# A decoder layer on one core: norms with a negated mean, and fewer products of ones at the start

## The chip, the cores and the metric

The kernel runs on one core of a Trainium2 chip. The metric is the device time of one execution in microseconds (us), as the median of several runs; lower is better. The core has five engines that run side by side, each in its own order: TensorE (PE; its weight loads are listed apart as PEld), VectorE (DVE), ScalarE (ACT), GpSimd (POOL) and SyncE (SP), whose work here is to issue DMAs. ACT issues a few DMAs too. Semaphores hold the engines together.

## The reference

One decoder layer over x of shape (4, 512, 128), all in float32: causal self-attention with 16 heads of 8, cross-attention over a context of 77 rows, and a mixture of 8 experts of which each token takes 2. A norm without gain or bias stands in front of each of the three.

```
def _layernorm(x, axis=-1, eps=1e-05):
    m = jnp.mean(x, axis=axis, keepdims=True)
    v = jnp.var(x, axis=axis, keepdims=True)
    return (x - m) / jnp.sqrt(v + eps)
...
x = x + attn(_layernorm(x), Wq, bq, Wk, bk, Wv, bv, Wp, bp)          # causal, softmax
x = x + xattn(_layernorm(x), ctx, ctx, mask, Wq, Wk, Wv, Wo)         # softmax over 77
x = x + ffn(_layernorm(x), gate_W, gate_b, expert_W, expert_b)       # top 2 of 8, /2
```

So there are 3 norms for each of 4 batches, 12 in all.

## The kernel before

**Layout.** A batch (b) is 512 tokens, in T = 4 tiles of 128 tokens on the partitions with 128 features in a row. `state` holds x for all batches and takes every residual sum. PSUM is one tensor `banks` of 8 banks; a step of the schedule gets one bank or two.

**Order of the work.** Each step is a triple (kind, b, k). `chains()` writes the steps as chains, one letter each: "a" is the first half of batch 0 (first_stats, first_norm, first_turn, first_q, first_k, first_split_q, first_split_k, then project_v and add_bias), "q" the same for its second half, "b", "c", "d" the norm and projections of batches 1 to 3, "e" to "h" the peaks (row maxima of the scores) of batches 0 to 3, "s" the scores, "v" the values, and so on. The string `ORDER` names which chain takes its next step; each engine walks through the same list `SCHEDULE` and issues what a step asks of it. So the string sets the order on all engines, and no engine passes a step that it waits in. The letter "w" is a step of its own, `warm`: one product of ones, 128x512 in bf16, into a bank that nobody reads (line 893). It takes time on PE alone and keeps it busy.

**A norm.** For a step ln_stats (11 of the 12 norms) DVE takes bn_stats of the four tiles (line 740) and bn_aggr (line 743), which leave mean and variance side by side in `moments`, and signals `moments_ready`. POOL adds epsilon to the variance (`var`, line 483) and raises it to the power of minus one half (`rstd`, line 484). For ln_norm POOL makes `normed`, tile by tile, in one tensor_scalar with two column operands (line 493):

```
for t in range(T):
    last = gp.tensor_scalar(normed[:, i % 2, t], state[:, b, t], moments[:, n, t, 0:1],
                            rstd[:, n, t:t + 1], ALU.subtract, ALU.mult)
```

PE then turns the four tiles (turn_x, line 884), ACT copies them out as `normed_t` (line 613), and the projections follow. The first norm of batch 0 is split in two halves of two tiles: DVE's statistics (lines 748 and 751), POOL's `var` and `rstd` (lines 472 and 473), and the two tiles by DVE for half 0 (line 757), by POOL for half 1 (line 477).

**The start.** POOL fills `ones_b` (line 438) and PE begins with 29 warm products, since these stand ahead of the first turn (first_turn, line 912) in the string. Then come the turn of half 0, 2 more, first_q of half 0 (line 918), the turn of half 1, first_k of half 0, 1 more, first_q of half 1, 2 more, first_k of half 1, project_v (line 877), the context's keys (line 896) and 30 more. ACT and DVE split q and k into bf16 parts (lines 621 to 627, 766, 773), SP and ACT copy these by DMA into `q_stack` and `k_stack` (line 339), and the peaks begin: products (lines 962 and 967) that DVE reduces to maxima (line 781). The scores (line 1008) wait for those maxima to be turned, copied (line 662) and written into `q_stack` by SP (line 415). SP issues all its DMAs in the order of the steps.

Of the kernel before, what the change touches and what calls it, by code (L numbers as in the profile page):

```python
# [11 lines left out]
ALU = mybir.AluOpType  # L12
# [3 lines left out]
B, S, D, H, E = 4, 512, 128, 16, 8  # L16
DH = D // H
S2 = 77
T = S // 128
# [5 lines left out]
LN_EPS = 1e-5  # L25
# [26 lines left out]
def chains():  # L52
# [37 lines left out]
    "aqaqPVPPPwwwwwwwwwwwwwwwwwwwwwwwwwwwwwaLLLbwwaPLqaPwqwwaqbaVcqaqKwwwwwwwwwwwwwwwwwwwwwwwwwwwwwweeebe"  # L90
    "cebebebPebwweeewwbcKeewKKeKwwweeKiewwwwwKeeicecefwsLesiwwsfsfsafswfisfsfsfsvfsvfssvvfsjsvvmbsfsdvjsf"
    "svfscvvfsfvsfdsmvmcffscmdfsfmvfjsmsmLmvsggjvsgvsgmgsgmgsgvsmgvsgndggksdgvsgsvAkAsvAsnsAvgsAvAdsgvnAs"
    "AnAsggvdgnsgvsgAsvgsknshsnvcxhxvxkhxvhoynxhxyxhnEhshnhxhdsholsEnshsvlhsyshsvvBsBdyBPEsBvBPsEsBvBBBvs"
    "hoEhshoBEshsvEoEshxoxhsovxohxyxhxyFxvloElsoEsxFEvsvosssvpyyssvvFspsvCsFsCvCCCvvpCCFCEpFzCFzpCtpFptzx"
    "xtxpxzypFxxypFxFxGytGpyttGGFwwwwzwwwwDtDGDDtDDwDDDGzGtzDtztxGGxxGxGyxxyxxtHytyHtHGHwwzHztHtHztzHwwww"
    "wHwwwHHtttwwwwwwwwwwwwwwHwwwwzztttztztttt"
# [76 lines left out]
def decoder_layer(nc, x, ctx_t, mask, wq, bq, wk, bk, wv, bv, wp, bp, xwq, xwk, xwv, xwo,  # L173
                  gate_w, gate_b, expert_w, expert_b, out):
    with ExitStack() as stack:
        def sb(name, shape, dt=F32):
            return stack.enter_context(nc.sbuf_tensor(name, shape, dt))
# [28 lines left out]
        moments = sb("moments", [128, 3 * B, T, 2])  # L206
        var = sb("var", [128, 3 * B, T])
# [221 lines left out]
        def _(pool):  # L429
            gp = nc.gpsimd  # L430
# [36 lines left out]
            for step in SCHEDULE:  # L467
                kind, b, k = step
                if kind == "first_stats":
                    t = slice(2 * k, 2 * k + 2)  # L470
                    pool.wait_ge(first_moments_ready, k + 1)
                    link(gp.tensor_scalar(var[:, 0, t], moments[:, 0, t, 1], LN_EPS, None, ALU.add))
                    gp.tensor_tensor(rstd[:, 0, t], var[:, 0, t], minus_half[:, t], ALU.pow).then_inc(first_rstd_ready, 1)
                elif kind == "first_norm" and k == 1:
                    pool.wait_ge(first_rstd_ready, 2)
                    for t in (2, 3):
                        last = gp.tensor_scalar(normed[:, 0, t], state[:, 0, t], moments[:, 0, t, 0:1],
                                                rstd[:, 0, t:t + 1], ALU.subtract, ALU.mult)
                    last.then_inc(first_norm_ready[k], 1)
                elif kind == "ln_stats":  # L480
                    n = 3 * b + k
                    pool.wait_ge(moments_ready, STATS[step])
                    link(gp.tensor_scalar(var[:, n], moments[:, n, :, 1], LN_EPS, None, ALU.add))  # L483
                    link(gp.tensor_tensor(rstd[:, n], var[:, n], minus_half[:], ALU.pow))  # L484
                elif kind == "ln_norm":
# [6 lines left out]
                    for t in range(T):  # L492
                        last = gp.tensor_scalar(normed[:, i % 2, t], state[:, b, t], moments[:, n, t, 0:1],  # L493
                                                rstd[:, n, t:t + 1], ALU.subtract, ALU.mult)
# [210 lines left out]
        def _(dve):  # L705
# [10 lines left out]
            for step in SCHEDULE:  # L716
# [16 lines left out]
                elif kind == "ln_stats":  # L733
# [10 lines left out]
                    last.then_inc(moments_ready, 1)  # L744
# [384 lines left out]
```

## Time and profile before

| | before |
|---|---|
| median of 3 runs | 279.18 us |
| lowest and highest run | 278.38, 280.30 us |
| the profiled execution, device time | 278.69 us |
| its span, first to last instruction | 277.0 us |
| busy: PE, DVE, ACT, POOL | 258.9, 207.6, 162.7, 150.5 us |
| TensorE clock granted, mean | 0.994 |
| chain that ended last: PE, DVE, POOL, ACT | 64%, 17%, 11%, 3% |

The span is 1.7 us shorter than the device time of the same execution. The chain that ended last is followed back from the last instruction, at each step to what released it or to the instruction before it on its engine. An engine's idle time is put down to whatever ended it.

### The profile page before, as it was taken

The page shows a single profiled execution, that of the slowest core. Times are in us where ns is not written, and L with a number is a line of the kernel's source. Part 1 is how long each engine was busy: PE and PEld are TensorE (multiplying, and loading weights), DVE is VectorE, ACT ScalarE, POOL GpSimd, SP SyncE. Part 2 cuts the span into 40 slices and gives each one's busy share as a digit, 9 for nine tenths or more (in the row PEclk, how much of TensorE's full clock was granted, in tenths as well). Part 3 has the DMA queues.
Part 4 walks back from the last instruction along what each step waited for, and adds up shares of the span by engine and source line. Part 5 has one row for each costly group of instructions (what it writes and reads, how often), then busy time and mean ns, then how long its engine had stood idle before and what let it go on. Part 6 is the DMA issues. An engine that isn't in the chain of part 4 may idle for free.

```text
span 277.0 us, 6747 instructions
## 1 busy us (share of the span) xinstructions
PE 258.9 (93%) x2642; PEld 140.3 (51%) x2642; DVE 207.6 (75%) x406; ACT 162.7 (59%) x223; POOL 150.5 (54%) x266
## 2 busy tenths in 40 slices
PE   8999896899988999999999969999799999998993
PEld 2554442434544444453545525367455684586583
DVE  6489997867887989987979945899338973864651
ACT  4232624989866988799977979961592009501100
POOL 7999833758869665675667694625811070032000
PEclk9999999799999999999999999999999999999999
DMA  3453364000452313400310001300004100100101
GB/s 106 110 143 94 86 165 110 2 6 4 117 152 71 82 37 105 135 9 5 100 31 2 7 2 29 98 2 8 0 11 116 38 7 2 38 2 0 38 2 39
DMA packets 21635, 14.62 MB, mean 53 GB/s; under 512 B 2788, under 2 KB 21604, under 8 KB 21604
## 3 DMA queue, kind: packets, MB, share of 16 engines
q1 hardware_dynamic: 20324, 13.61, 18.1%
q10 hardware_dynamic: 1280, 0.59, 0.8%
q8 instruction: 21, 0.34, 0.5%
q14 instruction: 10, 0.08, 0.1%
HBM read 2.39 MB, written 1.05 MB: 12 GB/s over the span
## 4 chain that ended last, share of the span: by engine, by line
PE 64%; DVE 17%; POOL 11%; ACT 3%; issue 2%; DMA 1%; POOLq 0%; SPq 0%; ACTq 0%
PE banks L1024 12%; POOL normed L493 8%; PE banks L1087 7%; PE banks L893 7%; PE banks L1008 7%; DVE peaks L781 6%; PE banks L884 5%; PE banks L967 4%; PE banks L1046 4%; PE banks L877 4%; PE banks L962 3%; DVE xpeaks L788 3%; POOL rstd L484 2%; PE banks L1073 2%; PE banks L1035 2%
## 5 line engine op out<-in xcount | busy, mean ns | idle before, releaser
L781 DVE TENSOR_REDUCE peaks<-banks 128x2 f32<-128x1024 f32 (+3 forms) x88 | 95.2, 1122 | 16.4 <-PE banks L967 15.8
L672 ACT ACTIVATE probs<-banks 128x1024 f32<-128x1024 f32 x80 | 79.4, 1031 | 14.3 <-PE banks L1008 13.7
L569 POOL TENSOR_SCALAR_AFFINE_SELECT probs<-probs 128x512 f32<-128x512 f32 (+1 forms) x80 | 43.2, 545 | 35.2 <-ACT probs L672 35.1
L1024 PE MATMUL banks<-probs,v_s 128*32 128x256 f32 (+3 forms) x512 | 43.2, 440 | 0.0
L677 ACT ACTIVATE xprobs<-banks 77x1024 f32<-77x1024 f32 x32 | 31.0, 1017 | 9.7 <-PE banks L1035 9.6
L493 POOL TENSOR_SCALAR normed<-state,moments,rstd 128x128 f32<-128x128 f32 x44 | 35.0, 809 | 0.7
L893 PE MATMUL banks<-ones_b 128*128 128x512 bf16 x118 | 32.1, 411 | 2.4 <-POOL minus_half L439 1.4
L1008 PE MATMUL banks<-q_stack,k_stack 64*128 64x512 bf16 (+3 forms) x256 | 30.8, 306 | 3.0 <-DMA q_stack<-peaks_t 2.4
L1087 PEld LDWEIGHTS banks<-expert_w_s,scaled 128*128 128x128 f32 x256 | 29.6, 192 | 4.9 <-issue 4.6
L1087 PE MATMUL banks<-expert_w_s,scaled 128*128 128x128 f32 x256 | 32.1, 280 | 0.0
L967 PE MATMUL banks<-k_stack,q_stack 64*128 64x512 bf16 (+3 forms) x256 | 31.9, 301 | 0.0
L851 DVE TENSOR_TENSOR scaled<-banks,normed_t 128x1024 f32<-128x1024 f32 x16 | 19.4, 1218 | 10.5 <-PE banks L1073 10.4
L962 PE MATMUL banks<-causal,halves 64*128 64x128 bf16 (+3 forms) x352 | 26.0, 227 | 1.0 <-DVE peaks L781 0.8
L788 DVE TENSOR_REDUCE xpeaks<-banks 128x8 f32<-128x616 f32 x32 | 23.9, 792 | 1.9 <-PE banks L983 1.6
L962 PEld LDWEIGHTS banks<-causal,halves 64*128 64x128 bf16 x352 | 13.3, 96 | 23.2 <-DVE peaks L781 10.4
L893 PEld LDWEIGHTS banks<-ones_b 128*128 128x128 bf16 x118 | 11.7, 104 | 17.4 <-issue 5.5
L1024 PEld LDWEIGHTS banks<-probs,v_s 128*32 128x32 f32 x512 | 12.3, 108 | 15.5 <-issue 11.4
L1008 PEld LDWEIGHTS banks<-q_stack,k_stack 64*128 64x128 bf16 x256 | 9.9, 96 | 16.3 <-DVE peaks L781 4.8
L1046 PE MATMUL banks<-xprobs,xv_s 77*32 77x512 f32 x128 | 16.6, 602 | 0.0
L613 ACT COPY normed_t<-banks 128x512 f32<-128x512 f32 x11 | 6.2, 586 | 16.3 <-PE banks L884 16.3
L807 DVE TENSOR_TENSOR g_scores<-banks,gate_b_s 128x32 f32<-128x32 f32 x4 | 0.8, 192 | 19.1 <-PE banks L877 19.1
L483 POOL TENSOR_SCALAR var<-moments 128x4 f32<-128x4 f32 x11 | 2.7, 246 | 22.4 <-DVE moments L743 22.3
(172 smaller groups left out, 370.8 us busy)
## 6 DMA issues: line engine op xcount, KB each, us to landing
xq_stack<-parts_x SPq DMA_DIRECT2D x24, 128.0 KB, 2.4
q_stack<-parts_q SPq DMA_DIRECT2D x18, 128.0 KB, 2.5
k_stack<-parts_k SPq DMA_DIRECT2D x18, 128.0 KB, 2.5
out<-state SPq DMA_DIRECT2D x4, 256.0 KB, 2.2
state<-in_x SPq DMA_DIRECT2D x3, 256.0 KB, 2.9
q_stack<-parts_q SPq DMA_DIRECT2D x12, 64.0 KB, 2.0
expert_w_s<-in_expert_w SPq DMA_DIRECT2D x1, 512.0 KB, 4.4
xk_stack<-parts_x SPq DMA_DIRECT2D x6, 77.0 KB
```

Source lines behind the costliest of these rows:

```text
L493: last = gp.tensor_scalar(normed[:, i % 2, t], state[:, b, t], moments[:, n, t, 0:1], rstd[:, n, t:t + 1], ALU.subtract, ALU.mult)
L569: gp.affine_select(out=v, in_=v, compare_op=ALU.is_ge, fill=0.0, base=0, pattern=pattern, channel_multiplier=-1).then_inc(causal_done, 1)
L672: ac.activation(probs[:, grp % 2, u], two_banks(step), ACT.Exp, scale=SCALE).then_inc(taken_by_act, 1)
L677: ac.activation(xprobs[0:S2, n % XPROBS], two_banks(step)[0:S2], ACT.Exp, scale=SCALE).then_inc(taken_by_act, 1)
L781: ve.tensor_reduce(peaks[:, f, t, :, a:a + n], two_banks(step)[:, :, 0:n * width].rearrange("p s (h k) -> p s h k", h=n), X_AXIS, ALU.max, ...
L788: ve.tensor_reduce(xpeaks[:, t, :, a:a + n], two_banks(step)[:, :, 0:n * S2].rearrange("p s (h k) -> p s h k", h=n), X_AXIS, ALU.max, nega ...
L893: te.matmul(bank(step), ones_b[:, 0:128], ones_b[:], start=True, stop=True)
L962: te.matmul(diagonal[:, s, :, 64 * i:128], halves[r, i], causal[r, 0:n, 0:128 - 64 * i], start=(i == 0), stop=False, skip_group_check=True)
L967: last = te.matmul(two[:, s, width * h:width * h + width], q_stack[r, b % 2, 4 * f + a + h, 128 * t:128 * t + 128], k_stack[r, b % 2, 4 * ...
L1008: last = te.matmul(two[:, s, col:col + n], k_stack[r, b % 2, p, 128 * kt:128 * kt + 128], q_stack[r, b % 2, p, 128 * kt:S], start=True, st ...
L1024: last = te.matmul(home[32 * c:32 * c + 32, 128 * kt:S], weight.rearrange("p a b -> p (a b)"), probs[:, half, unit, c % 2, col:col + S - 1 ...
L1087: last = te.matmul(home[:, D * t:D * t + D], scaled[:, (4 * b + k) % SCALED, i, 128 * t:128 * t + 128], expert_w_s[:, 2 * k + i], start=Fa ...
```

## The change

It has three parts. First, the norms that POOL makes add a negated mean in place of subtracting the mean: a new tile `shift` holds the means times -1, and line 493's operation (495 in the changed kernel) reads state, `shift` and `rstd` with ALU.add and ALU.mult. Second, for the 11 norms of ln_stats DVE makes both `shift` and the sum of variance and epsilon, `var`, behind its bn_aggr, after a wait for the last of these, and signals `moments_ready` with `var`; POOL no longer makes `var` there. In first_stats POOL still makes `var`, and for half 1 `shift` too. DVE's own two tiles of half 0 still subtract. Third, `ORDER` has 14 products of ones ahead of the first turn where it had 29, none between first_q and first_k of half 1 where it had 2, 4 behind the first three peaks, and 2, 1 and 2 more in three late places: 110 in all where it had 118. All other letters stand in the same order.

```
@@ ORDER @@
-    "aqaqPVPPPwwwwwwwwwwwwwwwwwwwwwwwwwwwwwaLLLbwwaPLqaPwqwwaqbaVcqaqKwwwwwwwwwwwwwwwwwwwwwwwwwwwwwweeebe"
+    "aqaqPVPPPwwwwwwwwwwwwwwaLLLbwwaPLqaPwqaqbaVcqaqKwwwwwwwwwwwwwwwwwwwwwwwwwwwwwweeewwwwbecebebebPebwwe"
...
+        shift = sb("shift", [128, 3 * B, T])
...
                 if kind == "first_stats":
                     t = slice(2 * k, 2 * k + 2)
                     pool.wait_ge(first_moments_ready, k + 1)
+                    if k == 1:
+                        gp.tensor_scalar(shift[:, 0, t], moments[:, 0, t, 0], -1.0, None, ALU.mult)
                     link(gp.tensor_scalar(var[:, 0, t], moments[:, 0, t, 1], LN_EPS, None, ALU.add))
...
                     for t in (2, 3):
-                        last = gp.tensor_scalar(normed[:, 0, t], state[:, 0, t], moments[:, 0, t, 0:1],
-                                                rstd[:, 0, t:t + 1], ALU.subtract, ALU.mult)
+                        last = gp.tensor_scalar(normed[:, 0, t], state[:, 0, t], shift[:, 0, t:t + 1],
+                                                rstd[:, 0, t:t + 1], ALU.add, ALU.mult)
...
                     pool.wait_ge(moments_ready, STATS[step])
-                    link(gp.tensor_scalar(var[:, n], moments[:, n, :, 1], LN_EPS, None, ALU.add))
                     link(gp.tensor_tensor(rstd[:, n], var[:, n], minus_half[:], ALU.pow))
...
                     for t in range(T):
-                        last = gp.tensor_scalar(normed[:, i % 2, t], state[:, b, t], moments[:, n, t, 0:1],
-                                                rstd[:, n, t:t + 1], ALU.subtract, ALU.mult)
+                        last = gp.tensor_scalar(normed[:, i % 2, t], state[:, b, t], shift[:, n, t:t + 1],
+                                                rstd[:, n, t:t + 1], ALU.add, ALU.mult)
...
                     for t in range(T):
                         last = ve.bn_aggr(moments[:, n, t], stats[:, n, t])
-                    last.then_inc(moments_ready, 1)
+                    link(last)
+                    ve.tensor_scalar(shift[:, n], moments[:, n, :, 0], -1.0, None, ALU.mult)
+                    ve.tensor_scalar(var[:, n], moments[:, n, :, 1], LN_EPS, None, ALU.add).then_inc(moments_ready, 1)
```

On PE, at the program's start, this stood before (ident and normed are the turns, ones_b the products of ones):

```order
L893 MATMUL banks<-ones_b 128x512 x29
L912 MATMUL banks<-ident,normed 128x128 x2
L893 MATMUL banks<-ones_b 128x512 x2
L918 MATMUL banks<-normed_t,wq_s 128x256
L912 MATMUL banks<-ident,normed 128x128 x2
L918 MATMUL banks<-normed_t,wk_s 128x256
L893 MATMUL banks<-ones_b 128x512
L918 MATMUL banks<-normed_t,wq_s 128x256
L893 MATMUL banks<-ones_b 128x512 x2
L918 MATMUL banks<-normed_t,wk_s 128x256
```

And this stands there in the changed kernel, whose lines are numbered 4 higher:

```order
L897 MATMUL banks<-ones_b 128x512 x14
L916 MATMUL banks<-ident,normed 128x128 x2
L897 MATMUL banks<-ones_b 128x512 x2
L922 MATMUL banks<-normed_t,wq_s 128x256
L916 MATMUL banks<-ident,normed 128x128 x2
L922 MATMUL banks<-normed_t,wk_s 128x256
L897 MATMUL banks<-ones_b 128x512
L922 MATMUL banks<-normed_t,wq_s 128x256
L922 MATMUL banks<-normed_t,wk_s 128x256
```

Fifteen products are gone ahead of the first turn and two ahead of the last first_k; the rest keeps its order.

On DVE, at the statistics of batch 1 near the start, this stands in the changed kernel:

```order
L742 BN_STATS stats<-state 128x6 x4
L745 BN_AGGR moments<-stats 128x2 x4
L747 TENSOR_SCALAR shift<-moments 128x4
L748 TENSOR_SCALAR var<-moments 128x4
L770 SCALAR_TENSOR_TENSOR full_q<-banks,bq_s,parts_q 128x256
```

Before, full_q stood right behind the BN_AGGR. On POOL the same norm and the next one read, before:

```order
L483 TENSOR_SCALAR var<-moments 128x4
L484 TENSOR_TENSOR rstd<-var,minus_half 128x4
L513 MEMSET zeros_b 24x512
L513 MEMSET expert_b_s 32x512
L493 TENSOR_SCALAR normed<-state,moments,rstd 128x128 x4
L483 TENSOR_SCALAR var<-moments 128x4
L484 TENSOR_TENSOR rstd<-var,minus_half 128x4
```

and in the changed kernel:

```order
L486 TENSOR_TENSOR rstd<-var,minus_half 128x4
L515 MEMSET zeros_b 24x512
L515 MEMSET expert_b_s 32x512
L495 TENSOR_SCALAR normed<-state,shift,rstd 128x128 x4
L486 TENSOR_TENSOR rstd<-var,minus_half 128x4
```

The `var` of each norm has gone from POOL to DVE, 11 times.

## Rows read from the trace of the kernel before

**Rows 1.** Chain that ended last, in order of time (start us, us, what)
```profile
1.37 9.33 PE banks L893 x29
...
12.08 0.22 PE banks L912 x2
...
47.12 0.39 PE banks L1008 x2
```
**Rows 2.** Instructions in order of time, 5 to 24 us (start us, us, engine line)
```profile
6.25 1.59 POOL L477 TENSOR_SCALAR normed<-state,moments,rstd 128x128 f32<-128x128 f32 x2
...
7.30 2.90 PEld L893 LDWEIGHTS banks<-ones_b 128*128 128x128 bf16 x14 [0.26 <-issue]
...
8.65 0.38 DVE L743 BATCH_NORM_AGGREGATE moments<-stats 128x2 f32<-128x6 f32 x4
...
12.62 0.48 DVE L766 SCALAR_TENSOR_TENSOR full_q<-banks,bq_s,parts_q 128x256 f32<-128x256 f32 x1 [3.60 <-ACT parts_q L621]
...
15.72 6.64 PE L893 MATMUL banks<-ones_b 128*128 128x512 bf16 x30
...
18.57 3.75 POOL L493 TENSOR_SCALAR normed<-state,moments,rstd 128x128 f32<-128x128 f32 x4
...
23.05 3.48 DVE L781 TENSOR_REDUCE peaks<-banks 128x8 f32<-128x1024 f32 x3
...
23.71 0.66 PE L884 MATMUL banks<-ident,normed 128*128 128x128 f32 x4
```
**Rows 3.** Busy time by stretch (us, PE, PEld, DVE, ACT, POOL, PEclk, DMA share, GB/s)
```profile
23.00:38.00 15.00, 13.52 (x144) 7.08 (x140) 14.99 (x16) 6.92 (x15) 11.43 (x14) 1.00 0.34 90
50.00:51.00 1.00, 1.00 (x14) 0.65 (x10) 0.91 (x1) 0.88 (x2) 0.77 (x4) 0.50 0.07 16
```
**Rows 4.** SP's queue in order of time, 12 to 46 us
```profile
12.66 3.83 SPq L339 DMA_DIRECT2D q_stack<-parts_q  x6
...
44.27 1.54 SPq L415 DMA_DIRECT2D q_stack<-peaks_t  x2
```
**Rows 5.** Who waited for whom (us in total, times, longest us)
```profile
PE banks L884 <- POOL normed L493: 6.3, 6, 2.0
```
**Rows 6.** Groups of POOL by form (count | busy us, mean ns | idle before)
```profile
L493 POOL TENSOR_SCALAR normed<-state,moments,rstd 128x128 f32<-128x128 f32 x44 | 35.0, 809 | 0.7
L530 POOL TENSOR_TENSOR state<-state,bias 128x512 f32<-128x512 f32 x4 | 5.1, 1270 | 0.1
L458 POOL TENSOR_TENSOR full_q<-full_q,parts_q 128x512 f32<-128x512 f32 x3 | 3.5, 1155 | 5.4 <-ACT full_q L648 5.4
L441 POOL TENSOR_SCALAR_AFFINE_SELECT ident<-ident 128x128 f32<-128x128 f32 x1 | 0.3, 296 | 0.2 <-POOL ident L440 0.2
```
**Rows 7.** A norm's hand-over from DVE to POOL, 154 to 157 us
```profile
154.80 0.38 DVE L743 BATCH_NORM_AGGREGATE moments<-stats 128x2 f32<-128x6 f32 x4
...
155.27 0.23 POOL L483 TENSOR_SCALAR var<-moments 128x4 f32<-128x4 f32 x1
...
155.59 1.04 POOL L484 TENSOR_TENSOR rstd<-var,minus_half 128x4 f32<-128x4 f32 x1
```
**Rows 8.** DVE and POOL in the gate's step, 204 to 210 us
```profile
204.79 0.18 DVE L809 TENSOR_SCALAR g_scores<-g_scores 128x32 f32<-128x32 f32 x1
205.01 0.19 DVE L811 TENSOR_REDUCE g_max<-g_scores 128x4 f32<-128x32 f32 x1
...
208.38 1.16 POOL L464 TENSOR_TENSOR parts_x<-full_x,parts_x 128x512 bf16<-128x512 f32 x1 [2.29 <-ACT parts_x L652]
...
208.66 0.92 DVE L828 TENSOR_TENSOR g_tied<-g_left,g_top 128x32 f32<-128x32 f32 x1
```
**Rows 9.** PE at the late turns of norms (200 to 252 us)
```profile
200.07 1.06 PE L884 MATMUL banks<-ident,normed 128*128 128x128 f32 x8 [1.49 <-POOL normed L493]
...
229.09 0.63 PE L884 MATMUL banks<-ident,normed 128*128 128x128 f32 x4 [0.18 <-POOL normed L493]
...
251.31 0.66 PE L884 MATMUL banks<-ident,normed 128*128 128x128 f32 x4 [0.76 <-POOL normed L493]
```

More of the change, by code:

```diff
@@ L89 @@
 ORDER = (
-    "aqaqPVPPPwwwwwwwwwwwwwwwwwwwwwwwwwwwwwaLLLbwwaPLqaPwqwwaqbaVcqaqKwwwwwwwwwwwwwwwwwwwwwwwwwwwwwweeebe"
[L91 to L96, printed above, removed]
+    "aqaqPVPPPwwwwwwwwwwwwwwaLLLbwwaPLqaPwqaqbaVcqaqKwwwwwwwwwwwwwwwwwwwwwwwwwwwwwweeewwwwbecebebebPebwwe"
+    "eewwbcKeewKKeKwwweeKiewwwwwKeeicecefwsLesiwwsfsfsafswfisfsfsfsvfsvfssvvfsjsvvmbsfsdvjsfsvfscvvfsfvsf"
+    "dsmvmcffscmdfsfmvfjsmsmLmvsggjvsgvsgmgsgmgsgvsmgvsgndggksdgvsgsvAkAsvAsnsAvgsAvAdsgvnAsAnAsggvdgnsgv"
+    "sgAsvgsknshsnvcxhxvxkhxvhoynxhxyxhnEhshnhxhdsholsEnshsvlhsyshsvvBsBdyBPEsBvBPsEsBvBBBvshoEhshoBEshsv"
+    "EoEshxoxhsovxohxyxhxyFxvloElsoEsxFEvsvosssvpyyssvvFspsvCsFsCvCCCvvpCCFCEpFzCFzpCtpFptzxxtxpxzywwpFxx"
+    "ypFxFxGytGpyttGGFwwwwzwwwwDtDGDDtDDwDDDGzGtzDtztxGwGxxGxGyxxyxxtHytyHtHGHwwzHztHtHztzHwwwwwwwHwwwHHt"
+    "ttwwwwwwwwwwwwwwHwwwwzztttztztttt"
 )
```

## The prediction

> **What bounds the kernel now.** I read the chain of waits first, from its start. After POOL has filled the ones it is PE alone for 9.33 us: 29 products of ones, until the first turn at 10.70 [rows 1]. The instructions in order of time then tell whether anything needs that time, and it does not: the later of the two half norms ends at 7.84 (6.25 and 1.59) [rows 2]. So the first turn stands behind products that nobody reads. From there the chain goes over ACT and DVE to the peaks. The stretches show who holds the stage that follows: DVE is busy for 14.99 of 15 us from 23 on [rows 3], and SP issues its copies one behind the other from 12.66 on, up to the two at 44.27 that bring the maxima and that the first scores at 47.12 wait for [rows 1, 4]. Both start from the first q and k. From about 50 us on PE is the main bound, with one kind of wait that bears on this change: it sat idle 6.3 us in six places for a norm by POOL [rows 5].
>
> **Fewer products in front.** The last 14 of the 29 weight loads take 2.90 us, 0.21 each; the 15 products ahead of them fill the time from 1.37 to about 7.3, 0.40 to 0.43 us each [rows 1, 2]. 512 columns in 0.43 us are the level of 1.2 GHz, in 0.21 that of 2.4 GHz; the rise came at about 7.3 us, with PE busy without a break before it. Fourteen products at the low level end at 1.37 + 14 x 0.427 = 7.34 us, where the first turn stood at 10.70: 3.36 us earlier. The data are there: the turn of half 1 goes from 12.08 to 8.7, against a norm that ends at 7.84, plus 0.23 for POOL's new `shift` by the row of `var`; the half of DVE is ready before that [rows 1, 2, 7]. On DVE the first q will be ready to take at about 12.62 - 3.36 = 9.26; the row of the aggregation ahead of it ends at 9.03 [rows 2], and with the two new instructions 9.3, so nothing is lost there. The two products gone between q and k of half 1 could give 0.43 us more; I count nothing, as ACT and DVE still take the halves one after the other there.
>
> DVE's second new pair, at the statistics of batch 2, lies in the loaded stretch and costs 0.25 (below). So the peaks begin near 23.05 - 3.36 + 0.25 = 19.9 us, 3.1 us earlier. The 30 products of ones in front of them, which ended at 22.36 (15.72 and 6.64), shift with the rest and end near 19.0 [rows 2]. SP's queue starts its first copy about 3.3 us earlier. What is late next is POOL, which does not move with PE: its norm of batch 1 ends at 22.3 (18.57 and 3.75) while PE turned it at 23.71 [rows 2]. After the change PE wants it at about 21.5, behind the 4 new products, which so lie in a wait and cost nothing. If POOL keeps its pace, PE gets the fourth peak out at 23.1 to 23.6, when DVE has just finished the third (19.9 + 3.48): a stall of 0.3 at most. I take 3.1 us; the bounds are 2.5 (POOL holds up more than that) and 3.4.
>
> **The norm itself.** 44 tiles at 809 ns mean [rows 6], four to a norm, so 3.2 us. The trace shows no addition of this form. From above it is the same instruction at the same 809 ns, and since nothing but the arithmetic differs it might be slower by as much as the addition on two tensors is over the subtraction, 1270 to 1155 ns for 512 elements: 0.9 us. From below it is the one-input pass over the same shape, 296 ns. Two tensors cost 1155 ns for 512 elements, about 1.9 ns an element over a fixed 0.2; the norm reads one tensor and pays (809 - 230) / 128 = 4.5 ns an element, out of line with every other row of POOL. Something in this form is slow, and the arithmetic is one of few candidates. I take 0.55 us, midway between 296 and 809, as an estimate: 0.25 us a tile, 1.0 us a norm. The six waits of PE are 2.0 us at most, the three late ones 1.49, 0.18 and 0.76, which leaves 1.9 for the other two [rows 5, 9]; 1.0 off each, but no more than there is (1.8 of the 1.9), gives 4.7 us. The late new products take some back: 1 of 0.21 where the wait was 0.18, and 2 of 0.43 where it was 0.76; the 2 at the wait of 1.49 fit in what is left of it [rows 9]. That leaves 4.0 us, and since the chain is off PE for 36% of the span, so that behind such a wait another engine is often the next bound, I count half: 2.0 us. The bounds are 0 and 4.5.
>
> **The sum by DVE.** DVE gets 22 instructions. One behind a wait for the one before it starts 0.22 us later (204.79 to 205.01) and takes 0.18 [rows 8]; the second of a pair follows without a wait, as the four aggregations do in 0.38 together [rows 7]. So a pair is 0.25 to 0.28 us, 3 us in all on DVE. The hand-over: the aggregation ended at 155.18, `rstd` began at 155.59, so 0.41 us with POOL's `var` between; in its place stand 0.28 and the 0.09 of the signal, 0.37. The delay to the norm is the same. Queued behind the pair on DVE is mostly a reduction of peaks, for which PE waits in turn. The chain had 17% of the span on DVE, so of 3 us I charge about that share, 0.4 us with the one in front already counted. Bounds are 0 and 2: an instruction of DVE with two tensors took 0.92 us in place of 0.19 beside a running instruction of POOL [rows 8], and POOL is busy for half the span, so half of 11 pairs might lose 0.7, of which half on the chain.
>
> The Trainium skill (SBUF — State Buffer, "Who interferes with whom") says that a tensor_scalar of VectorE can take the port pair that GpSimd uses, and that whoever comes second waits for the whole instruction. The trace agrees for two tensors (0.92 us), and has no tensor_scalar of DVE on so small a tile beside a busy POOL; by the rule the term would be nearer to its upper bound, and the time 1 to 1.5 us above my sum.
>
> **The sum.** The profiled execution took 278.69 us. Less 3.1, less 2.0, plus 0.4 is 274.0. The median of the runs is 0.49 above the profiled one, so 274.5 us.
>
> **The rivals.** (1) The addition costs what the subtraction does. For it: it is the same instruction, and on two tensors the addition is not the cheaper one [rows 6]. Then 278.69 - 3.1 + 0.4 = 276.0, and 276.5 on the scale of the median; the new products lie in the waits that stay. The Trainium skill (GPSIMD Engine Reference, "Elementwise — side-by-side cycle accounting") prices a loop by how many operations it has for an element and knows no dearer subtraction: by that rule this is the case.
>
> (2) The addition runs like a plain pass, 0.3 to 0.4 us a tile. For it is the row of 296 ns. Each norm is then 1.6 to 2 us shorter; nearly all of the 6.3 us goes, less 0.6 for the new products, and at two thirds 3.7 in place of 2.0: 272.8 us.
>
> (3) The front turns against the kernel, on the clock. The products of ones brought the clock up at 7.3 us, and 14 end at 7.34, so the next work is sparser before it is sure that the rise has come. If it has not, PE's work between the first turn at 10.70 and the 30 products at 15.72, 4.6 us without the 2 products removed, takes up to 8.6, and half of the 30 cost 0.21 us more each: 7.2 us lost against 3.36 gained. The peaks then start at about 26.3 in place of 23.05, and the sum is 278.69 + 3.2 - 1.6 = 280.3, 280.8 on the scale of the median, slower than before. It decides from the point where the rise comes 3.1 us of PE time late. Against it: PE goes on nearly without a gap, as it did from 10.70 before, and the clock held then; it fell later, after an idle time, to 0.50 at 50 us [rows 3]. The Trainium skill (TensorE: Matmul & The Clock Gate, "The HAM clock gate") says that the throttled state is the default and that the point of release differs from run to run; the trace shows the first, one profile cannot show the second.
>
> (4) The front's gain is given back in the loaded stretch, since SP or POOL gets its inputs no earlier: of 3.1 us one remains. Against it: POOL is busy for 11.43 of 15 us between 23 and 38 [rows 3], so it can catch up. With the half-counted norm gain that is 276.6 us.
>
> **How the numbers follow.** The forecast has 0.38, rival 1 0.28, rival 2 0.20, rival 3 0.05, rival 4 0.09. The range leaves out rival 3 and a part of rival 2: 271.6 to 277.5. About 1% is what a measurement tells from no change, 2.8 us here, a bound at 276.4. Faster by over 1% are the forecast, rival 2, and somewhat under half of rivals 1 and 4, which lie on the bound: 0.38 + 0.20 + 0.16 = 0.74, and a little more as the forecast itself has margin: 0.75. Slower by over 1% is a part of rival 3, 0.03. The rest, 0.22, is within 1%.
>
> **What would show it.** The profile after should have the first turn at about 7.4 us, the first reduction of peaks at 19.9 and the first scores' product at 43.9 where it stood at 47.1. The group of `normed` on POOL shows the price of the addition at once: 0.55 is my case, 0.8 rival 1, under 0.4 rival 2. The waits of PE for `normed` should fall from 6.3 us to about 2. If products of ones still stand 0.43 us apart behind the first turn, rival 3 is at work; if the reductions start early but have gaps for PE between them, rival 4. A pair of the new instructions that takes over 0.5 us would mean that POOL holds up DVE. I am wrong in kind if the first scores come no earlier than before.

## The result and the profile after

| | before | changed |
|---|---|---|
| median, us | 279.74 (4 runs) | 270.89 (4 runs) |
| lowest and highest, us | 278.38, 282.40 | 270.74, 272.19 |
| profiled execution, device time, us | 278.69 | 270.91 |
| its span, us | 277.0 | 269.1 |
| busy: PE, DVE, ACT, POOL, us | 258.9, 207.6, 162.7, 150.5 | 254.5, 210.1, 163.0, 131.7 |

The ratio is 0.968 (95% interval 0.960 to 0.976): 8.9 us less, where 4.7 less was forecast (274.5), and below the stated range. The sign was right, the size was about half.

The page of the changed kernel, engines and chain:

```profile
PE 254.5 (95%) x2622; PEld 139.1 (52%) x2634; DVE 210.1 (78%) x428; ACT 163.0 (61%) x223; POOL 131.7 (49%) x256
...
PE 70%; SPq 13%; DVE 10%; issue 2%; ACT 1%; POOL 1%; DMA 1%; POOLq 0%; ACTq 0%
```

POOL fell from 11% of the chain to 1%, and SP's queue, which had no share to speak of, has 13%. The groups of POOL in the changed kernel (as in [rows 6]):

```profile
L495 POOL TENSOR_SCALAR normed<-state,shift,rstd 128x128 f32<-128x128 f32 x44 | 19.1, 448 | 0.7
L486 POOL TENSOR_TENSOR rstd<-var,minus_half 128x4 f32<-128x4 f32 x11 | 11.2, 1019 | 26.5 <-DVE var L748 26.0 <-PE banks L1039 0.5
```

A tile takes 448 ns in place of 809: 1.44 us less for each norm. The row of PE's waits for `normed` [rows 5], 6.3 us before, is gone from the list of waits: what is left of PE's waits for a norm is 0.15 us at the start, for the tiles of half 1.

The start, in order of time (start, us, engine, line, operation), which answers to [rows 2]:

```profile
1.38 5.01 PE L897 MATMUL banks<-ones_b 128*128 128x512 bf16 x14 [1.38 <-POOL minus_half L440]
...
6.22 0.38 PE L916 MATMUL banks<-ident,normed 128*128 128x128 f32 x2
...
7.92 0.41 PE L916 MATMUL banks<-ident,normed 128*128 128x128 f32 x2 [0.15 <-POOL normed L480]
...
18.41 1.78 POOL L495 TENSOR_SCALAR normed<-state,shift,rstd 128x128 f32<-128x128 f32 x4
...
19.33 5.73 DVE L785 TENSOR_REDUCE peaks<-banks 128x8 f32<-128x1024 f32 x5
```

The 14 products end at 6.4 (1.38 and 5.01), not at 7.34. The weight loads tell why: they are 0.43 us apart up to 5.14 us and closer from there, so the clock rose at 5.1 us in this execution and at 7.3 in the one before. The first reduction of peaks begins at 19.33 in place of 23.05.

Where the time went is best read from marks that both kernels share, above all DVE's sums into `state`. Each column is the mark of that kernel's profiled execution, in us; the last two are experiments described below. Of five kernels with the fast norm and the late products (the changed one, 29 and 8 in front, the wait filled, SP's copies moved), the time from the 1st sum to the last is 186.24 to 186.26 us in every profile, so there the marks tell tenths of a microsecond that the medians can't. (The two kernels with other instructions on POOL have 186.11 and 186.81.)

| mark | before | changed | norm edits alone | changed, SP's copies moved |
|---|---|---|---|---|
| first reduction of peaks | 23.05 | 19.33 | 22.14 | 19.48 |
| first copy of maxima issued by SP | 44.27 | 42.25 | 44.26 | 39.28 |
| first scores' product | 47.12 | 45.09 | 47.11 | 42.29 |
| 1st sum into state | 81.84 | 79.58 | 80.77 | 76.03 |
| 2nd | 118.68 | 115.30 | 116.48 | 111.74 |
| 5th | 187.67 | 182.62 | 183.80 | 179.06 |
| 7th | 212.89 | 206.69 | 207.49 | 203.14 |
| 10th | 244.57 | 238.37 | 239.16 | 234.82 |
| 11th | 259.89 | 253.15 | 253.50 | 249.59 |
| last | 272.58 | 265.84 | 266.19 | 262.28 |
| end of the span | 277.0 | 269.1 | 269.5 | 265.6 |

So the front gave 2.0 us by the first scores, the rest of the kernel 4.7 more, and 1.1 lies behind the last sum, where the last store landed sooner: SP waited 1.8 us for it, and 2.9 before. Nothing forecast that, and its cause is open: the wait is 1.8 us in all 12 profiles of kernels in which DVE makes `shift`, and 2.4 in the one with the new order alone.

### The profile page after: what moved, and what is told of

Same layout as the page of the kernel before. It is cut to its first block, busy times and chain, and to the rows that moved or that the text cites. A ratio compares the mean times of both kernels' runs of the same rounds, so it can differ in the third digit from the quotient of the medians.

```text
span 269.1 us, 6731 instructions
## 1 busy us (share of the span) xinstructions
PE 254.5 (95%) x2622; PEld 139.1 (52%) x2634; DVE 210.1 (78%) x428; ACT 163.0 (61%) x223; POOL 131.7 (49%) x256
## 4 chain that ended last, share of the span: by engine, by line
PE 70%; SPq 13%; DVE 10%; issue 2%; ACT 1%; POOL 1%; DMA 1%; POOLq 0%; ACTq 0%
PE banks L1028 13%; PE banks L1091 10%; SPq L340 9%; PE banks L1012 7%; PE banks L888 6%; PE banks L881 5%; PE banks L1050 5%; PE banks L971 4%; PE banks L897 4%; PE banks L966 4%; DVE peaks L785 4%; PE banks L1077 3%; PE banks L1039 2%; PE banks L987 2%; PE banks L939 2%
## 5 line engine op out<-in xcount | busy, mean ns | idle before, releaser
L897 PE MATMUL banks<-ones_b 128*128 128x512 bf16 x98 | 27.0, 406 | 3.3 <-POOL minus_half L440 1.4
L486 POOL TENSOR_TENSOR rstd<-var,minus_half 128x4 f32<-128x4 f32 x11 | 11.2, 1019 | 26.5 <-DVE var L748 26.0
L495 POOL TENSOR_SCALAR normed<-state,shift,rstd 128x128 f32<-128x128 f32 x44 | 19.1, 448 | 0.7
L897 PEld LDWEIGHTS banks<-ones_b 128*128 128x128 bf16 x110 | 10.4, 102 | 16.5 <-issue 4.5
```

The source lines that it names most:

```text
L897: te.matmul(bank(step), ones_b[:, 0:128], ones_b[:], start=True, stop=True)
```

## The experiments

All times below are medians; "before" was run again beside each set, at 280.5, 280.2 and 281.2 us, so the ratios to it are the surer numbers.

**Norm edits alone** (the new norm and hand-over, the old string with 29 products in front).

```
-ORDER of the changed kernel
+ORDER of the kernel before
```

> The kernel before with the norm edits alone (shift, add, sum by DVE) and the old order with 29 products in front. Theory A (two gains that add up: front 2.1 us at the first scores, norms some 4.7 us later, seen as the rest of the shift between the two profiles): about 275 us, norm tile 0.45 us, first scores near 47.1 us as before. Rival (the gain is mostly the front, the norm only lets it through): about 278 us.

Measured: 271.96 us, ratio 0.974 (0.969 to 0.980), profiled execution 271.25. The marks are in the table. This is 3 us below theory A's 275: the norm alone brings most of the whole result. At the last sum it is 6.4 us ahead of the kernel before, of which about 0.8 has another cause (the clock, below). Seen the other way round, the new order adds 1.1 us to the norm edits by the medians, and 0.3 in the profiled executions (271.25 and 270.91).

**New order alone** (the new string, norms as before).

```
-ORDER of the kernel before
+ORDER of the changed kernel
```

> The kernel before with the new order alone, norms untouched. Theory A: about 277 us; tile at 0.80 us; first scores 2 to 3 us earlier than 47.1. Rival 4 of the prediction (POOL at its old pace holds up the loaded stretch and gives the front's gain back): 279 us and first scores at 46 or later.

Measured: 281.16 us over 10 runs from 277.8 to 282.5, ratio 0.999 (0.994 to 1.003): nothing. Its first scores stood at 45.28, 1.8 us early, so the front's gain was there, and the rival's reason (POOL holds up the loaded stretch) is not what took it. The stretches show what did (columns as in [rows 3]):

```profile
150.00:160.00 10.00, 9.98 (x103) 5.01 (x102) 9.50 (x25) 9.06 (x11) 7.24 (x13) 1.00 0.02 7
164.00:174.00 10.00, 9.29 (x40) 5.72 (x44) 1.86 (x6) 5.81 (x9) 3.90 (x8) 0.50 0.02 5
```

Ten microseconds at a granted clock of 0.50. They begin in this wait of PE for a norm at the old pace:

```profile
164.72 1.51 PE L884 MATMUL banks<-ident,normed 128*128 128x128 f32 x6 [2.04 <-POOL normed L493]
```

The same wait of 2.0 us stands in the profile before, without a fall of the clock there. The executions of this kernel differ by their mean granted clock: the three at 0.988 took 277.8 to 278.6 us, the seven at 0.966 to 0.981 took 280.1 to 282.5. So a front gain of about 1.5 us exists where the clock holds, and behind the wait for the norm it was lost in the profiled one.

**Subtraction again**, all else as in the changed kernel.

```
-state[:, b, t], shift[:, n, t:t + 1], rstd[:, n, t:t + 1], ALU.add, ALU.mult
+state[:, b, t], moments[:, n, t, 0:1], rstd[:, n, t:t + 1], ALU.subtract, ALU.mult
```

> The changed kernel with one thing undone: the 44 tiles of POOL subtract the mean from moments again; DVE still makes shift (now read by nobody there) and var. If the arithmetic alone sets the tile's price: tile back at 0.80 us and about 277 us, like the order alone give or take the hand-over by DVE (0.3 us). If the price came from reading the mean out of the pairs in moments or from the idle time of POOL: it stays at 0.45.

Measured: 276.23 us, ratio 0.990 (0.987 to 0.994). The group in its profile:

```profile
L495 POOL TENSOR_SCALAR normed<-state,moments,rstd 128x128 f32<-128x128 f32 x44 | 34.8, 803 | 0.7
```

The arithmetic alone sets the tile's price, and it is worth 5.3 us by the medians (276.23 to 270.89), 6 by the ratios (0.990 to 0.968), in this order. The expected 277 held within 0.8. From the kernel with the new order alone this one differs only by the hand-over and the first half norm of POOL, and yet its median is 4.9 us lower. Part of that is the clock: among the executions at 0.988 alone the medians are 278.59 and 276.23 us, 2.4 apart. PE waits 4.3 us for norms here and 6.6 there. So with the slow norm the hand-over may be worth something; no run tells more.

**Forms of tensor_scalar on POOL.** 26 more operations behind the last one of POOL, each behind a wait for the one before it, on a tile of their own.

```
+for _ in range(2):
+    gp.tensor_scalar(probe_in[:, 0:128], probe_in[:, 0:128], probe_col[:, 0:1], probe_col[:, 1:2], ALU.add, ALU.mult)
+    gp.tensor_scalar(probe_in[:, 0:128], probe_in[:, 0:128], probe_col[:, 0:1], probe_col[:, 1:2], ALU.subtract, ALU.mult)
...
```

> The changed kernel with 26 more operations on POOL behind its last one, on a tile of their own, 13 forms of tensor_scalar twice each. If subtraction as such is dear on POOL: add with mult 0.44 us for 128 elements, subtract with mult 0.79, mult with subtract about 0.79 too, whether the columns lie side by side or in pairs and whether they are columns or constants. If it is the order of the operations (subtract first): mult with subtract at 0.44. Slope from 128 to 512 elements: about 1.7 ns an element for add, 4.4 for subtract. One step (subtract alone) shows which part the second step has.

Measured, in the order in which the program has them: add and mult (line 579), subtract and mult (580), mult and add (581), mult and subtract (582), mult and mult (583), add and subtract first with the columns lying in pairs (584, 585), the same two with constants (586, 587), add alone and subtract alone with one column (588, 589), add and subtract first on 512 elements (590, 591).

```profile
L579 POOL TENSOR_SCALAR probe_in<-probe_in,probe_col x2: 447/447/447, 244.5 to 255.0; 128x128 f32<-128x128 f32 x2
...
L580 POOL TENSOR_SCALAR probe_in<-probe_in,probe_col x2: 792/802/811, 245.0 to 255.6; 128x128 f32<-128x128 f32 x2
...
L581 POOL TENSOR_SCALAR probe_in<-probe_in,probe_col x2: 449/449/449, 245.9 to 256.4; 128x128 f32<-128x128 f32 x2
...
L582 POOL TENSOR_SCALAR probe_in<-probe_in,probe_col x2: 802/802/803, 246.5 to 257.0; 128x128 f32<-128x128 f32 x2
...
L585 POOL TENSOR_SCALAR probe_in<-probe_in,probe_pair x2: 802/812/822, 248.5 to 259.0; 128x128 f32<-128x128 f32 x2
...
L586 POOL TENSOR_SCALAR probe_in<-probe_in x2: 297/298/298, 249.4 to 259.9; 128x128 f32<-128x128 f32 x2
...
L587 POOL TENSOR_SCALAR probe_in<-probe_in x2: 643/643/643, 249.8 to 260.3; 128x128 f32<-128x128 f32 x2
...
L588 POOL TENSOR_SCALAR probe_in<-probe_in,probe_col x2: 606/612/619, 250.5 to 261.0; 128x128 f32<-128x128 f32 x2
...
L590 POOL TENSOR_SCALAR probe_in<-probe_in,probe_col x2: 762/762/762, 251.9 to 262.4; 128x512 f32<-128x512 f32 x2
...
L591 POOL TENSOR_SCALAR probe_in<-probe_in,probe_col x2: 2072/2086/2100, 252.8 to 263.3; 128x512 f32<-128x512 f32 x2
```

The numbers are the shortest, median and longest duration in ns. Every pair of add and mult takes 450 ns, every pair with a subtract in it 800, in either place; the pairs of `moments` do not matter. From 128 to 512 elements the first grows by 315 ns (0.8 ns an element), the second by 1284 (3.3). I had expected 1.7 for the addition: it has a larger fixed part, some 0.34 us, of which the constants' row at 298 saves nearly half. For the subtraction I had expected 4.4. A single addition with a column costs more (612) than an addition and a product together, and there a subtraction is no dearer (603, line 589): it is the pair with a subtract in it that is slow. This kernel was run once.

**29 products in front** of the changed kernel.

```
-"aqaqPVPPP" + 14 * "w" + "aLLLb..."
+"aqaqPVPPP" + 29 * "w" + "aLLLb..."
```

> The changed kernel with 29 products of ones in front of the first turn again, all else as changed. Theory A: first turn at about 9.6 to 10.7 us and the time some 2 to 3 us above the changed kernel, 273 to 274 us. Rival (the front's gain is lost again before 47 us because SP's queue is the bound there): less than 1 us, 271.5.

Measured: 273.63 us (271.18 to 273.92), ratio 0.978 (0.971 to 0.984), 2.7 above the changed kernel. First turn at 9.9, first scores at 47.17, so 2.1 us of this is the front, as in theory A.

**8 products in front.**

```
-"aqaqPVPPP" + 14 * "w" + "aLLLb..."
+"aqaqPVPPP" + 8 * "w" + "aLLLb..."
```

> The changed kernel with 8 products of ones in front of the first turn. They end at about 4.8 us, and the first turn waits for its norm until 5.9. If the clock rises by then all the same: like the changed kernel, at most 0.3 us less, 270.8. By rival 3 of the prediction (the work behind the products is too sparse to bring the clock up): products between 6 and 11 us stand 0.43 us apart, the first reduction of peaks comes 1 to 3 us later than 19.3, and the time is 272 to 274 us.

Measured: 272.51 us (270.81 to 274.18), ratio 0.973 (0.966 to 0.979). PE at the start:

```profile
1.37 3.59 PE L897 MATMUL banks<-ones_b 128*128 128x512 bf16 x8 [1.37 <-POOL minus_half L440]
6.00 0.41 PE L916 MATMUL banks<-ident,normed 128*128 128x128 f32 x2 [1.04 <-DVE normed L761]
6.25 0.59 PE L897 MATMUL banks<-ones_b 128*128 128x512 bf16 x2
```

The two products behind the turn take 0.21 us each, so the clock was up by 6.2 us here even with an idle microsecond in front, and the first reduction began at 19.30, as in the changed kernel. Rival 3 did not come about in this execution. Nothing is gained either, since the turn of half 1 waits for POOL until 7.9. What the profiled execution lost, it lost at 43 to 49 us, at a clock of 0.50.

**The sum of variance and epsilon on POOL again.**

```
 pool.wait_ge(moments_ready, STATS[step])
+link(gp.tensor_scalar(var[:, n], moments[:, n, :, 1], LN_EPS, None, ALU.add))
...
-ve.tensor_scalar(var[:, n], moments[:, n, :, 1], LN_EPS, None, ALU.add).then_inc(moments_ready, 1)
```

> The changed kernel with the sum of variance and epsilon made by POOL again; DVE still makes shift. If the hand-over costs what I worked out (0.37 us by DVE against 0.41 by POOL alone): with shift still on DVE's way the norm starts 0.3 us later than in the changed kernel, and as no wait of PE for a norm was left, the time rises by under 0.8 us, 271.3. If DVE's pair had been a burden on the path: it falls.

Measured: 271.73 us (270.08 to 273.95), ratio to before 0.970 (0.965 to 0.976) against 0.968 for the changed kernel. With the norm fast, this part cannot be told from nothing. The hand-over itself came out as reckoned: from the end of the aggregation to the start of `rstd`, where POOL was free, it is 0.41 us in the kernel before, 0.36 in the changed one (forecast 0.37) and 0.61 here.

**No late products.**

```
-...xpxzywwpFxx...DtztxGwGxxG...tztzHwwwwwwwHwww...
+...xpxzypFxx...DtztxGGxxG...tztzHwwwwwHwww...
```

> The changed kernel without the 5 late products of ones (2, 1 and 2). Theory A (with the faster norm PE no longer waits there, so each lies on PE's path at 0.21 us): the last stretch of the shift comes back, about 0.85 to 1.0 us less than the changed kernel, 270.0 us. Rival (they only fill waits): same as the changed kernel, 270.9.

Measured: 271.41 us (270.79 to 272.96), ratio 0.970 (0.966 to 0.975), no gain over the changed kernel. In its profile the clock fell a second time:

```profile
186.00:189.00 3.00, 3.00 (x16) 3.00 (x16) 2.63 (x9) 0.00 (x0) 2.37 (x5) 0.54 0.06 16
```

The missing products can't be the cause. The first two of the five stand at 193.7 us in the changed kernel, just ahead of the turns (which this kernel reaches at 195.63), and up to there PE's list is the same. Nor had PE been idle: from the first scores to 186 us it has no gap above 0.5 us. The stretch from the 5th sum to the 7th, in which the fall lies, is 25.31 us here and 24.07 in the changed kernel; from the 10th to the 11th, where two more of the products are gone and the clock is up, it is 14.33 for 14.78.

**The wait ahead of the first scores filled.**

```
-...eicecefwsLesiww...
+...eicecefw + 15 * "w" + sLesiww...
```

> The changed kernel with 15 more products of ones in PE's wait of 4.0 us ahead of the first scores. Theory A (after that wait the clock falls to half for 3.4 us, which costs about 0.8 us later): no low stretch between 45 and 51 us, about 0.8 us less, 270.1. Rival (PE is not the bound there, so the low clock is free): same as the changed kernel; or, if the products run past the wait, up to 0.5 us more.

Measured: 270.21 us (269.45 to 272.88), ratio 0.969 (0.963 to 0.974). The stretches of the changed kernel and then of this one, from 44 us:

```profile
44.00:46.00 2.00, 0.91 (x11) 0.41 (x12) 0.18 (x1) 0.48 (x1) 0.00 (x0) 1.00 0.39 116
46.00:49.00 3.00, 3.00 (x26) 1.54 (x28) 1.82 (x2) 2.83 (x4) 1.65 (x7) 0.51 0.05 14
```

```profile
44.00:46.00 2.00, 1.66 (x17) 0.57 (x17) 0.77 (x1) 1.07 (x2) 0.00 (x0) 1.00 0.47 131
46.00:49.00 3.00, 2.35 (x36) 1.19 (x32) 2.76 (x4) 3.00 (x4) 2.25 (x8) 1.00 0.03 5
```

In 46 to 49 us PE did 36 products in 2.35 us with the clock up, and 26 in 3.00 with it at half. From the first scores to the first sum it is 33.65 us here and 34.49 in the changed kernel: the low stretch behind a wait of 4.0 us of PE costs 0.84. That is the price in one pair of profiles: in five others with the fast norm and a low stretch there, the same way takes 34.83 to 35.24. The executions with a full clock took 269.5 to 270.8, two others 272.8 and 272.9. The gain is real in the profile, and at the edge of what the medians tell.

**Both of these.**

> Both edits together: no late products, and the wait ahead of the first scores filled. If the two gains add up: about 269.2 us; if they share a bound: 270.0.

Measured: 269.47 us (268.19 to 271.92), ratio 0.963 (0.958 to 0.968). They add up about as theory A said.

**SP's copies moved.** The profile of the changed kernel has the maxima ready at 37.75 us (37.18 and 0.57), but SP issued their copy only at 42.25, behind the context's keys:

```profile
37.18 0.57 ACT L664 COPY peaks_t<-banks 24x512 bf16<-24x512 bf16 x1 [2.74 <-PE banks L998]
...
38.39 3.81 SPq L340 DMA_DIRECT2D xk_stack<-parts_x  x6
...
42.25 1.54 SPq L416 DMA_DIRECT2D q_stack<-peaks_t  x2
...
45.09 0.39 PE L1012 MATMUL banks<-q_stack,k_stack 64*128 64x512 bf16 x2 [3.98 <-DMA q_stack<-peaks_t]
```

```
-elif kind == "split_context":
-    copy_parts(sp, "x", 1, K_PARTS, xk_stack, slice(0, B * S2), xk_stacked)
...
 elif kind == "turn_peaks":
     ...
+    if (b, k) == (0, 0):
+        copy_parts(sp, "x", 1, K_PARTS, xk_stack, slice(0, B * S2), xk_stacked)
```

> The changed kernel with one thing moved in SP's queue: the 6 copies of the context's keys into xk_stack go behind the first two copies of the maxima (peaks_t), which were ready at 37.75 us and left at 42.25. Theory B (SP's queue sets the first scores, and that is where 1.2 of the front's 3.3 us were lost): first copy of the maxima at about 38.5 us, first scores' product at about 41.3 in place of 45.1, no fall of the clock behind it, and 2.5 to 3.5 us less in all: 268 us. Rival (DVE or PE hold the stage behind the first scores, as DVE's reductions run to 42.4): first scores early, but under 1 us less at the end, 270.2.

Measured: 266.69 us (266.43 to 267.36), ratio 0.952 (0.950 to 0.955): 4.2 us below the changed kernel (3.6 in the profiled executions), more than expected. Its queue and PE:

```profile
34.29 4.94 SPq L340 DMA_DIRECT2D k_stack<-parts_k  x6
39.28 1.53 SPq L413 DMA_DIRECT2D q_stack<-peaks_t  x2
40.86 3.79 SPq L340 DMA_DIRECT2D xk_stack<-parts_x  x6
```

```profile
41.31 0.50 PE L965 MATMUL banks<-causal,halves 64*128 64x512 bf16 x4 [1.10 <-DMA k_stack<-parts_k]
41.64 0.40 PE L970 MATMUL banks<-k_stack,q_stack 64*128 64x128 bf16 x8
41.97 0.39 PE L896 MATMUL banks<-ones_b 128*128 128x512 bf16 x1
42.29 0.39 PE L1011 MATMUL banks<-q_stack,k_stack 64*128 64x512 bf16 x2
```

The first scores come 2.8 us earlier with no wait right before them (one of 1.10 us for `k_stack` stands a microsecond ahead), and the clock stays up until the end of the work in the profile (mean 1.00 in all six runs, where the changed kernel had 0.985 to 0.991), which gives some 0.75 besides (33.74 us from there to the first sum for 34.49). The six runs spread over 0.9 us. So theory B holds: SP's queue, and not DVE or PE, set the first scores.

**The move, and no late products.**

> The same move together with the 5 late products of ones left out. Theory B: the sum of both gains, 0.8 us less than with the move alone: 267.2 us. If the late products keep the clock up (it fell at 186 to 190 us in the profile of the kernel without them), there is no gain over the move alone.

Measured: 266.09 us (265.50 to 266.80), ratio 0.950 (0.947 to 0.953), 0.6 us below the move alone, and 0.81 in the profiles from the 1st sum to the last. It beats both kernels of this study, by 15 us and by 4.8.

## Why the prediction was right or wrong

**The price of the norm: right in kind, the estimate too high.** I took 0.55 us, midway between 296 and 809 ns; it is 0.448. Rival 1 (chance 0.28), which leaned on the row of the addition on two tensors, was wrong, and so was the rule cited from the Trainium skill (GPSIMD Engine Reference, "Elementwise — side-by-side cycle accounting") as far as I read it: 800 and 450 ns for the same number of operations an element show that it matters which operation it is, and the measurement decides. What pointed the right way was the sentence that 4.5 ns an element is out of line with every other row of POOL. Rival 2 (0.20) came nearest, at 272.8 us: its price of under 0.4 was a little too low, but nearly all of the waits went, as it said.

**"I count half": the step that failed.** PE had waited 6.3 us for norms. I let the faster norm take 4.0 of it, after the late products, and then halved that to 2.0, since another engine would often be the next bound. Hardly any was. These are the three of the six waits that [rows 9] does not show:

```profile
76.96 0.63 PE L884 MATMUL banks<-ident,normed 128*128 128x128 f32 x4 [0.73 <-POOL normed L493]
88.60 0.66 PE L884 MATMUL banks<-ident,normed 128*128 128x128 f32 x4 [1.15 <-POOL normed L493]
165.55 1.06 PE L884 MATMUL banks<-ident,normed 128*128 128x128 f32 x8 [2.00 <-POOL normed L493]
```

Take the norm edits alone, which have neither the new front nor the late products. Five of the waits, 5.58 us, lie between the 1st sum and the last, and that way takes 185.42 us in place of 190.74: 5.32 less. Stretch by stretch between the sums it is 1.13 for a wait of 1.15, 1.67 for 2.00, 1.53 for 1.49, nothing for 0.18 and 0.98 for 0.76. With the first wait it is 6.4 at the last sum, or 5.6 of 6.3 if the fall of the clock in the kernel before, which this execution did not have, cost the same 0.84 as in the changed kernel (an estimate). For the changed kernel the same 5.6 less 0.83 for the late products is 4.7, and with the front's 2.0 that is the 6.7 of the last sum in the table. Between first scores and last sum I had forecast 2.0 - 0.4 = 1.6 and got 4.7. These 3.1 us are three quarters of the miss of 4.2: 2.7 belong to the halved term and 0.4 to DVE's pairs, of which nothing showed. Within the halved term the price of a tile is the smaller part. With 1.44 us off each norm, and no more than the wait, the six waits give 5.7 in place of 4.7; had I halved that too, less the late products, I would have had 2.4.

The rows told it, had I used them place by place. The two largest waits went further than 1.44 us a norm allows, and this is why: each belongs to the second of two norms that stand close together on POOL. In the kernel before, the second one's aggregation ended at 159.79 us, but POOL was still at the first one's tiles and what had queued behind them:

```profile
159.82 1.02 POOL L569 TENSOR_SCALAR_AFFINE_SELECT probs<-probs 128x256 f32<-128x256 f32 x2
160.81 0.23 POOL L483 TENSOR_SCALAR var<-moments 128x4 f32<-128x4 f32 x1
161.13 1.04 POOL L484 TENSOR_TENSOR rstd<-var,minus_half 128x4 f32<-128x4 f32 x1
```

With the norm edits alone POOL is free and waiting:

```profile
158.12 1.02 POOL L486 TENSOR_TENSOR rstd<-var,minus_half 128x4 f32<-128x4 f32 x1 [0.41 <-DVE var L748]
```

From the aggregation's end to `rstd` it was 1.34 us there and is 0.36 here; at the pair near 190 us it was 1.94 and is 0.36. So the second norm of a pair gains 2.4 to 3.0 us, not 1.44. The chain's share of other engines over the whole span says nothing about these six places.

**The front: right up to the first peaks, a third lost at SP.** Every number up to there came out or better: first turn 6.22 (forecast 7.4), first reduction 19.33 (19.9). That the turn came so much earlier is luck: the clock rose 2.2 us earlier than I had carried over, and in the ten profiles whose kernels begin with these 14 products the first turn stands anywhere from 5.8 to 7.2 us. The first scores stand at 44.5 to 45.8 us in the eight of them in which SP's order is the old one, and at 47.1 to 47.2 in the three profiles with 29 products, so the front is worth 1.3 to 2.7 us there. The products of ones behind the peaks lay in a wait, as said, and POOL, now faster, held nothing up. But the first scores came at 45.09, not at 43.9. I had seen that SP issues its copies one behind the other up to the maxima, and took it that the queue would just shift. It had started 3.28 us earlier (9.38 for 12.66) and lost 1.26 on the way, in two places: three copies at 19.14 took 2.74 us where they had taken 1.88 to 1.90, and six at 33.82 took 4.53 where they had taken 3.8. In each a single issue lasted over 1.2 us. What held these is open. The new order is not needed for it: with the norm edits alone the queue started 1.34 us earlier than before (11.32), three copies at 21.09 took 3.20 us, and the maxima left at 44.26 as before. Each of the other 13 profiles has a single issue of over 1 us between 19 and 23 us; the kernel before has none there. The move in SP's queue shows that the queue was the bound.

**The two products between q and k** and the hand-over by DVE gave nothing to be measured, as forecast. The 0.4 us charged for DVE's pairs was too much: with the norm edits alone nothing of it shows at the sums. With the norm slow, the hand-over may have been a gain (above). The rule cited from the Trainium skill (SBUF — State Buffer, "Who interferes with whom") is borne out by what DVE did beside a memset. DVE's new instructions beside a running memset of POOL:

```profile
14.34 1.80 POOL L513 MEMSET xq_stack<- 128x2048 f32 x1
...
15.00 1.16 DVE L747 TENSOR_SCALAR shift<-moments 128x4 f32<-128x4 f32 x1
15.08 1.09 DVE L748 TENSOR_SCALAR var<-moments 128x4 f32<-128x4 f32 x1
15.15 1.02 DVE L777 TENSOR_TENSOR parts_q<-full_q,parts_q 128x256 bf16<-128x256 f32 x1
```

All three end at 16.17, right after the memset at 16.14. A `shift` takes 0.17 us in 8 of 11 places, and 0.42, 1.16 and 0.43 in three. The 1 to 1.5 us that I let the rule have did not come, since only three pairs met POOL at work. Nor is each such pair held: in the kernel with the subtraction again one came in the middle of the tiles of a norm on POOL and took no longer than by itself. There the measurement differs from the rule.

```profile
192.16 3.14 POOL L495 TENSOR_SCALAR normed<-state,moments,rstd 128x128 f32<-128x128 f32 x4
194.02 0.17 DVE L747 TENSOR_SCALAR shift<-moments 128x4 f32<-128x4 f32 x1
```

**The late products.** I counted 0.6 us for them, as the waits would shrink. In the marks they cost 0.83 from the 1st sum to the last: the kernel with norm edits alone, which lacks them, needs 0.38 us less between the 5th and 7th sums and 0.44 less between the 10th and 11th, where they stand, and the two kernels that leave them out and had no late fall of the clock show the same. The one whose clock fell at 186 us needs 1.24 more from the 5th to the 7th. With SP's copies moved it did not fall, and leaving them out gave 0.6 us. Whether the late products ever hold the clock up, no run shows.

**The clock.** Rival 3 (0.05) did not occur, with 14 products or with 8. The Trainium skill's sentence (TensorE: Matmul & The Clock Gate, "The HAM clock gate") that the point of release differs from run to run is borne out by 7.3 and 5.1 us in two profiles whose first 5 us are the same on PE. What I had not weighed is the clock later on. In every profile that left the wait ahead of the first scores as it was, the one before included, the clock fell to half there, at a cost of 0.84 us in the changed kernel; the norm edits alone are the exception. In the kernel with the new order alone it fell again for ten microseconds at 164 us: from the 2nd sum to the 5th it needs 73.31 us in place of 68.99, and the front's gain was 0.87 at the 1st sum. Rival 4 (0.09) had the order's gain nearly gone by another way, SP or POOL in the loaded stretch; of its 3.1 us, 2.0 were left at the first scores.

## What to carry to other kernels

When an operation that a busy engine waits for gets faster, sum min(saving, wait) over its places in the trace (the smaller of the two at each), not a share of it by the chain over the whole span. Here that gives 5.7 us, where the marks say 5.6. Where two such operations follow each other closely on the engine that gets faster, the second gains what the first gives up as well. A discount belongs only to a place where something else stands close behind; of the five places past the 1st sum one gave nothing back, and its wait was 0.18 us. Before you blame an edit for a change in the profile, look where the edit stands in time: one fall of the clock came 7 us ahead of the products that were left out. When an earlier start is to carry through a stage, follow the one queue that has no gap, and ask what stands in it ahead of the transfer that releases the next stage: here six copies that nobody needed for long stood in front of two that everybody waited for, and moving them was worth 4.2 us. On GpSimd, look at the time an element of each form; a subtraction in a tensor_scalar can be written as the addition of a negated column.

## What the runs showed of the hardware

- On POOL a tensor_scalar of 128x128 float32 with two column operands takes 447 to 450 ns with add and mult or mult and mult, and 802 ns as soon as one of the two is a subtract; with constants 298 and 643. With one column and one operation it takes 612 (add) and 603 (subtract), more than two operations.
- A tensor_scalar of DVE on 4 elements, 0.17 us by itself, took 1.16 us beside a memset of POOL and ended with it, and 0.43 beside an affine_select. Beside a tensor_scalar of POOL with two columns it took 0.17.
- The granted clock fell to 0.50 in or behind idle times of PE of 2.0 to 4.0 us, but not behind each: a wait of 3.3 us in the kernel with the norm edits alone and one of 2.0 us in the kernel before were followed by no fall. Once it fell (0.54 from 186 to 189 us) where PE had had no gap above 0.5 us since the first scores. Falls go with much of the spread, not with all of it: the two kernels with SP's copies moved, whose clock never fell, spread over 0.9 and 1.3 us in six runs, the kernel with the new order alone over 4.7 in ten; but three runs with the norm edits alone at the same mean clock of 0.994 lie 2.2 us apart.
- The column of the granted clock says 1.00 during the first 5 to 7 us, although the products there stand 0.43 us apart; the spacing is the surer sign at the start.
